# The sixteen experts' outputs in a fused vision/mixture kernel: one weighted running sum on VectorE instead of scaled copies on ScalarE and a tree of additions

## The reference

```python
logits = einsum('bsd,de->bse', x, gate_w) + gate_b
top_probs, top_idx = top_k(softmax(logits), 2)          # then divided by their sum
dispatch = sum(one_hot(top_idx, 16) * top_probs[..., None], axis=-2)   # 14 of 16 are zero
h1 = einsum('bsd,edh->bseh', x, w1)
h2 = einsum('bsd,edh->bseh', x, w2)
hidden = silu(h1) * h2                                  # 128 hidden units per expert
expert_out = einsum('bseh,eho->bseo', hidden, w3)
out = h + einsum('bseo,bse->bso', expert_out, dispatch) # x = layernorm(h)
```

## Time and profile before

| | us |
|---|---|
| median of 3 runs | 2467.79 (2460.09 to 2467.89) |
| the profiled execution, its own time | 2476.72 |
| its span, first to last instruction | 2474.9 |
| mean granted TensorE clock | 0.943 |

### The profile page before, as it was taken

One profiled execution on the slowest core, in us unless ns is written; L12 is line 12 of the kernel. 1 busy time (PEld: TensorE's weight loads), 2 busy tenths in 40 slices (PEclk: granted clock), 3 DMA queues, 4 the chain that ended last, 5 costly groups with the idle time before them and its releaser, 6 DMA issues.

```text
span 2474.9 us, 46859 instructions
## 1 busy us (share of the span) xinstructions
PE 2210.1 (89%) x15441; PEld 1979.4 (80%) x15441; DVE 1856.8 (75%) x4865; ACT 1399.1 (57%) x4344; POOL 1673.7 (68%) x2168
## 2 busy tenths in 40 slices
PE   2578989989999998999999899999999999989887
PEld 1566778888888888879889888888889888878776
DVE  1226888788788778888787878878787888887765
ACT  1124466566665656566565656656565666655555
POOL 0378887777686858868586877858686786867500
PEclk9967999999999999999899999989999999989989
DMA  9575636356472736538272745638173563712100
GB/s 221 148 207 154 182 104 186 113 164 173 110 217 66 213 97 177 167 106 222 77 212 85 198 138 152 186 95 225 52 221 108 166 175 109 201 52 68 49 3 6
DMA packets 362993, 346.85 MB, mean 140 GB/s; under 512 B 49152, under 2 KB 313472, under 8 KB 362624
## 3 DMA queue, kind: packets, MB, share of 16 engines
q1 hardware_dynamic: 313600, 209.57, 31.4%
q0 software_dynamic: 49152, 134.28, 18.6%
HBM read 205.87 MB, written 137.89 MB: 139 GB/s over the span
## 4 chain that ended last, share of the span: by engine, by line
PE 58%; issue 11%; DVE 11%; ACT 10%; POOL 8%; DMA 2%; ACTq 0%; DVEq 0%; another core or an unknown queue 0%; POOLq 0%
PE bank_o L634 16%; PE bank_h L624 8%; PE bank_d L700 7%; PE bank_h L625 7%; PE bank_d L690 7%; POOL gath L570 5%; ACT scaled L831 5%; PE bank_a L727 5%; PE bank_a L712 2%; POOL rest L577 2%; DMA gath<-table,idx 2%; DVE hid L967 2%; DVE wsam L1062 1%; PE bank_p L655 1%; PE bank_a L741 1%
## 5 line engine op out<-in xcount | busy, mean ns | idle before, releaser
L570 POOL DMA_INDIRECT gath<-table,idx x1024 | 1110.6, 1085 | 267.2 <-issue 238.5
L831 ACT ACTIVATE scaled<-bank_o,disp 128x64 f32<-128x64 f32 x2304 | 502.2, 330 | 370.8 <-PE bank_o L634 334.4
L624 PE MATMUL bank_h<-xsplit,w 128*128 128x384 f32 x1536 | 634.7, 413 | 83.3 <-ACT silu L780 52.9
L634 PEld LDWEIGHTS bank_o<-w_sb,hid 128*128 128x128 f32 x4608 | 567.9, 197 | 10.1 <-DVE hid L967 9.6
L634 PE MATMUL bank_o<-w_sb,hid 128*128 128x64 f32 x4608 | 563.8, 278 | 6.3 <-DVE hid L967 6.2
L625 PE MATMUL bank_h<-xsplit,w 128*128 128x384 f32 x1536 | 539.0, 351 | 0.0
L780 ACT ACTIVATE silu<-bank_h 128x384 f32<-128x384 f32 x768 | 393.8, 514 | 122.0 <-PE bank_h L625 104.2
L967 DVE TENSOR_TENSOR hid<-silu,bank_h 128x384 f32<-128x384 f32 x768 | 416.8, 548 | 53.4 <-ACT silu L780 38.5
L577 POOL MEMSET rest<- 1x400 f32 x1024 | 432.1, 422 | 29.6
L624 PEld LDWEIGHTS bank_h<-xsplit,w 128*128 128x128 f32 x1536 | 307.6, 200 | 139.5 <-ACT silu L780 68.0
L1062 DVE TENSOR_TENSOR wsam<-gath,cw 128x1024 f32<-128x1024 f32 x256 | 312.6, 1221 | 115.4 <-PE bank_d L690 54.7
(11 more groups left out here) (141 smaller groups left out, 2306.2 us busy)
## 6 DMA issues: line engine op xcount, KB each, us to landing
table<-pixmaj SPq DMA_DIRECT2D x80, 1024.0 KB
xin<-x_dram SPq DMA_DIRECT2D x256, 256.0 KB
table<-pixmaj SPq DMA_DIRECT2D x32, 960.0 KB
table<-pixmaj SPq DMA_DIRECT2D x16, 1088.0 KB
gath<-table,idx POOLq DMA_INDIRECT x1024
out_dram<-ob SPq DMA_DIRECT2D x48, 96.0 KB
gath<-w_dram SPq DMA_DIRECT2D x4, 512.0 KB, 8.8
interp_sb<-interp_dram SPq DMA_DIRECT2D x1, 1024.0 KB, 5.3
```

The costliest lines, as they stand in the source:

```text
L570: pool.indirect_dma_start(out=gath[buf][:, p, :, :].rearrange("p a c -> p (a c)"), out_offset=None, in_=table[par], in_offset=bass.Indirec ...
L624: mm(bank[:, 0:GC], w12[:, e, which, 0, :], xsplit[gp][:], start=True, stop=False)
L634: last = mm(bank_o[n % 2][:, C * i:C * (i + 1)], hid[:, e, 128 * k:128 * (k + 1)], w3_sb[:, e, :], start=True, stop=True)
L831: last = nc.scalar.activation(scaled[n % 2][:, i, :], bank_o[n % 2][:, C * i:C * (i + 1)], ACT.Identity, scale=disp[gpar(par, g)][:, k, e: ...
```

## The change

Each expert's output is handled by itself. As soon as its `hid` is there, PE makes the three tiles' outputs (three products of 64 columns) in one bank, and DVE runs three instructions of 64 columns, one per tile: output from PSUM times the dispatch weight (one number per token, read from `disp`) plus the running sum `ob`, written back to `ob`; for expert 0 the residual `h2` stands in place of the running sum. ACT has no part in it any more. `scaled`, `part`, M2 and their semaphores are gone; `hid` holds 4 experts' products instead of 16; `eo_added` counts the additions. The order strings of all five engines are new.

```diff
+HB = 4
-    ("W", "pe"): [(0, 0, 0), (0, 0, 1), (0, 0, 2), (0, 1, 0), (0, 1, 1), (0, 1, 2), (1, 0, 0), (1, 0, 1), (1, 0, 2), (1, 1, 0), (1, 1, 1), (1, 1, 2), (2, 0, 0), (2, 0, 1), (2, 0, 2), (2, 1, 0), (2, 1, 1), (2, 1, 2)],
+    ("W", "pe"): [(i, j) for i in range(3) for j in range(16)],
...
 ORDER = {
     "pe": (
...
-        "kFhlFlFEEFvEFaxFaaFaFFaaFEFEkFrEFkFslFtlFakFaFakFElFvlFEkFxEkFalFalFakFEFkaFlFErlFsaFEkaFtaFkblFblFE",
+        "FEtEaFbbkFElFElFbEbvFEbkFExFkbEbFlEbFlEcFEkFEdkFElFErlFsEFkEFEtkgFEhlFElFEaFEvFaEaFExEFaaFEaFaEaFEFE",
...
-        hid = sb("hid", [128, NE, GC])
-        scaled = [sb(f"scaled{i}", [128, 8, C]) for i in range(2)]
-        part = sb("part", [128, 2, GT, C])
+        hid = sb("hid", [128, HB, GC])
...
                     elif kind == "W":
-                        g, half, k = args
-                        n = 2 * GT * (NGRP * b + g) + GT * half + k
-                        pe.wait_ge(hid_done, SLOTS * b + NE * g + 8 * half + 8)
-                        wait(pe, eo_scaled, n - 1)
-                        for i in range(8):
-                            e = 8 * half + i
-                            last = mm(bank_o[n % 2][:, C * i:C * (i + 1)], hid[:, e, 128 * k:128 * (k + 1)],
+                        g, e = args
+                        n = SLOTS * b + NE * g + e
+                        pe.wait_ge(hid_done, n + 1)
+                        wait(pe, eo_added, GT * (n - 1))
+                        for k in range(GT):
+                            last = mm(bank_o[n % 2][:, C * k:C * (k + 1)], hid[:, n % HB, 128 * k:128 * (k + 1)],
                                       w3_sb[:, e, :], start=True, stop=True)
                         last.then_inc(eo_ready, 1)
...
-                    elif kind == "W":
-                        act.wait_ge(eo_ready, n + 1)
-                        act.wait_ge(disp_done, NGRP * b + g + 1)
-                        wait(act, pair_sum, n - 1)
-                        for i in range(8):
-                            e = 8 * half + i
-                            last = nc.scalar.activation(scaled[n % 2][:, i, :], bank_o[n % 2][:, C * i:C * (i + 1)],
-                                                        ACT.Identity, scale=disp[gpar(par, g)][:, k, e:e + 1])
-                        last.then_inc(eo_scaled, 1)
...
-                        if e % 8 == 0:
-                            wait(dve, eo_ready, 2 * GT * (NGRP * b + g - 1) + GT * (e // 8 + 1))
+                        wait(dve, eo_ready, n - HB + 1)
                         r = (2 * (NE * g + e) + 1) % 3
-                        tt(hid[:, e, :], silu[e % 2][:], bank_h[r][:, 0:GC], ALU.mult).then_inc(hid_done, 1)
+                        tt(hid[:, n % HB, :], silu[e % 2][:], bank_h[r][:, 0:GC], ALU.mult).then_inc(hid_done, 1)
                     elif kind == "Z":
-                        dve.wait_ge(eo_scaled, n + 1)
-                        eo = scaled[n % 2]
-                        for m in (4, 2):
-                            link(sums, tt(eo[:, 0:m, :], eo[:, 0:m, :], eo[:, m:2 * m, :], ALU.add))
-                        tt(part[:, half, k, :], eo[:, 0, :], eo[:, 1, :], ALU.add).then_inc(pair_sum, 1)
-                    elif kind == "M2":
-                        dve.wait_ge(pair_sum, 2 * GT * (NGRP * b + g + 1))
-                        wait(dve, out_done[gp], 8 * NGRP * b + 8 * (g - gp))
-                        link(mix, tt(ob[gp][:], part[:, 0, :, :], part[:, 1, :, :], ALU.add))
-                        tt(ob[gp][:], ob[gp][:], h2[g][:], ALU.add).then_inc(ob_done, 1)
+                        dve.wait_ge(eo_ready, n + 1)
+                        if e == 0:
+                            wait(dve, out_done[gp], 8 * NGRP * b + 8 * (g - gp))
+                        for k in range(GT):
+                            if e:
+                                dve.wait_ge(eo_added, GT * (n - 1) + k + 1)
+                            stt(ob[gp][:, k, :], bank_o[n % 2][:, C * k:C * (k + 1)], disp[gp][:, k, e:e + 1],
+                                (ob[gp] if e else h2[g])[:, k, :], ALU.mult, ALU.add).then_inc(eo_added, 1)
```

More of the change, by code:

```diff
@@ L119 @@
     ("L", "sp"): [(i,) for i in range(8)],
-    ("M2", "dve"): [(i,) for i in range(3)],
     ("M2", "sp"): [(i,) for i in range(3)],
@@ L152 @@
     ("X", "dve"): [(i, j) for i in range(3) for j in range(16)],
-    ("Z", "dve"): [(0, 0, 0), (0, 0, 1), (0, 0, 2), (0, 1, 0), (0, 1, 1), (0, 1, 2), (1, 0, 0), (1, 0, 1), (1, 0, 2), (1, 1, 0), (1, 1, 1), (1, 1, 2), (2, 0, 0), (2, 0, 1), (2, 0, 2), (2, 1, 0), (2, 1, 1), (2, 1, 2)],
+    ("Z", "dve"): [(i, j) for i in range(3) for j in range(16)],
 }
@@ new lines @@
+        "GxFCGyFGFqGjFGFGjrFsGFGjFGlFGlFmGtjuFGFGwFGjlFGlvmFjGFGxFGyFGljFqGlFmGFGjrFsGFGlFjlGmAFGBjFGtFuGFGCl",
+        "wlFmGjFGvFjGFGxFyGqFGljFrsGlmFGjFGdFGeFljGFlgmGFGjFGtuFGilFGwlFmGAFGvFGGBFxFCGyFGFqGjFGFGjrFsGFGjFGl",
+        "FGlmFGtjuFGFGwjFGlFGlvmFjGFGxFGyFGljFqGlFmGFGjrFsGFGFljlGmFAGFGtujFGBFlGCwlFmGjFGvFGjFGxFGyFGlFqjGlF",
+        "mGFGrFsGjFGFGFGlFjGltmuFGFGwFjGFGvFGFGlxlFmGAyFGBFCGqFGFGrFsGFGFGFGFGtuFGFGwFGFGvFGFGxFGyFGFqGFGFGrF",
+        "sGFGFGFGFGtuFGFGwFGFGvFGFGxFGyFGFGFGFGFGFGFGFGFGFGFGFGFGFGFGFGFGFGGG",
@@ L241 @@
-        "DppoozopozoozoozDppoozopozoozoozDppoozopozoozzDppppppppp",
+        "ooDDoozoozoozoozoozoozoozoozoooooozzzoozpDoooopzzpoozopDozpoozoozpoozpoozDpoozoozpoozpoozDpoozoozpoo",
+        "zpoozDpoozoozpoozpoozDpoozoozpoozpoozDpoozoozpoozpoozDpoozoozpoozpoozDpoozoozpoozpoozDpoozoozpoozpoo",
+        "zDpoozoozpoozpoozDpoozoozpoozpoozDpoozoozpoozpzDpppppppp",
     ),
@@ L475, in gpar @@
             return (NGRP * p + g) % 2
-        def n_odd(g, half, k):
-            return (2 * GT * g + GT * half + k) % 2
         @block.sync
@@ L506, in out_group @@
             def out_group(b, g, gp):
-                wait(sp, ob_done, NGRP * b + g + 1)
+                wait(sp, eo_added, GT * NE * (NGRP * b + g + 1))
                 dst = out[b]
@@ L910, in _ @@
             step(ts(c_st[:], c_st[:], col[:, 13:14], None, ALU.mult))
-            nc.vector.memset(part[:], 0.0).then_inc(setup_done, 1)
+            nc.vector.memset(hid[:, 0, 0:8], 0.0).then_inc(setup_done, 1)
             dve.wait_ge(setup_a, 6)
@@ L920, in _ @@
                                   Chain(top_s, NGRP * TOP_N))
[L922 removed]
+            skip = Chain(skip_v, NGRP * 2)
             def link(chain, ins):
@@ L1005, in run @@
                         dve.wait_ge(skip_v, 2 * NGRP * b + 2 * g + 2)
-                        wait(dve, ob_done, NGRP * (b - 1) + g + 1)
+                        wait(dve, eo_added, GT * (SLOTS * (b - 1) + NE * g + 1))
                         tt(h2[g][:], bank_p[:, 0:GT * C].rearrange("p (k c) -> p k c", k=GT),
@@ L1045, in run @@
                         link(top, ts(top_p[:, 3, :], top_p[:, 1, :], -0.5, 0.5, ALU.mult, ALU.add))
-                        wait(dve, eo_scaled, 2 * GT * (NGRP * b + g - 1))
+                        wait(dve, eo_added, GT * NE * (NGRP * b + g - 1))
                         top.inc(tt(disp[gp][:], spread(iota_e[:], 1, GT), spread(top_f[:, :, 0], 2, NE), ALU.is_equal))
```

167 lines of the change are left out of this document (78 added, 89 removed).

## The result

The changed kernel takes 2380.76 us (median of 4 runs, 2372.95 to 2384.32) against 2466.61 us of the kernel before (4 runs, 2460.09 to 2467.89): a ratio of 0.9653, 95% interval 0.9623 to 0.9682, or 86 us less. The forecast had the direction, but 31 us, and its range for the likeliest case (2405 to 2458) lies above the result; the wider range, 2380 to 2500, just holds it. The profiled execution took 2381.35 us and spans 2379.1, where the one before spans 2474.9.

The account below looks back on a forecast made before the run. PE was taken to bound the middle, and waits, not an engine, the tail. Middle -31 + 6 + 17 = -8 us and tail -23 gave -31 from the median 2467.8, so 2437 us; range 2380 to 2500.

Parts of the forecast that it names:

- The step that failed: Middle, PE: 79 more transitions from an output product to an expert step, 0.08 us each, +6 us.
- ACT's term: Middle: scaled copies gone, half of PE's waits for silu and the `v_sb` copy saved, -31 us (bounds 0 and 63).
- DVE's price: Weighted addition of 64 columns on DVE: lasts 0.284 us, 0.20 start to start (0.145 to 0.31); DVE busy about 2010.
- the wait for `eo_ready`: DVE before each set of additions, waiting for PE's products: little or none; above 7 us per image meant wrong.
- the second term that failed: Middle, DVE: +9.7 us work less 8.5 us waiting per image, +17 us at worst if all reached PE.
- The tail: After the last D3 product: 128.4 us shrinks to 105, -23 us (bounds -35 and 0).
- The clock term: End of the run: clock averaging 0.89 in the last 127 us adds 14 us to 84 us of work.
- ACT busy: Whole run, a sign to check: ACT busy about 900 us.
- Line 1142's successor: Middle, once-per-image line: expected every 141 to 142 us; under 139 meant the forecast was wrong.
- A: Whole kernel, the forecast itself: silu and evacuations prompt, DVE has room; 2405 to 2458 us, chance 0.46.
- D: Middle: PE's waits nearly vanish, an image takes 134 to 137 us; whole kernel 2335 to 2376 us, chance 0.14.
- C: Whole kernel: nothing moves, ACT's waits were hidden, DVE's longer list eats the end's gain; 2461 to 2475 us, chance 0.12.

Follow-up runs that it names:

- e2_act_copies: Changed kernel with ACT's three scaled copies per expert put back and one 192-column addition per expert on DVE: 2389.42 us, ratio 0.9677.
- e4b_act_filler_waits: Changed kernel plus three unused 64-column ACT instructions per expert, each set waiting for that expert's products on PE: 2445.07 us, ratio 0.9901.
- e4a_act_filler: Changed kernel plus three unused 64-column ACT instructions per expert, without a wait for PE's products: 2392.74 us, ratio 0.9693.
- b1_one_copy: Kernel before, old order, each round's eight scaled ACT copies replaced by one 512-column copy without dispatch weights: 2428.32 us, ratio 0.9836.
- c2_pairs: Changed kernel with two experts' outputs in a row on PE and their six additions in a row on DVE, eight `hid` buffers: 2430.74 us, ratio 0.9817.
- c4_fours: Changed kernel with four experts' outputs and their twelve additions in a row, 16 `hid` buffers, two experts per bank: 2554.77 us, ratio 1.0371.
- b2_no_act_copy: Kernel before, old order, no output copies on ACT; dispatch weights and half the outputs left out, DVE reads PSUM: 2441.14 us, ratio 0.9885.
- e5_dve_filler: Changed kernel plus one more weighted addition of 64 columns per expert on DVE, into a scratch tile: 2472.43 us, ratio 1.0035.
- h2_act_copies_later: e2_act_copies with each set of scaled copies 1.0 us later in ACT's string: 2434.42 us, ratio 0.9869 against the kernel before.

## Why the forecast was right and wrong, step by step

The chain before, e2_act_copies, e4b_act_filler_waits, changed takes the change apart: first the order and the size of the sets (ACT's copies stay; DVE's work becomes 53 us less); then the additions go to DVE (+211 us of DVE work, ACT about as loaded and still waiting for the products); then ACT's share goes away. Per image and for the tail, by the table:

| step | 13.8 images | of it with the clock (estimate) | tail | whole, by the ratios | forecast |
|---|---|---|---|---|---|
| order, small sets | -3.5 x 13.8 = -49 | +5 | -30 | -80 | +6 in the middle |
| additions on DVE | +3.7 x 13.8 = +51 | +20 | +2 | +55 | +17 in the middle |
| ACT free | -4.3 x 13.8 = -59 | -38 | -3 | -61 | -31 in the middle |
| sum | -57 | -13 | -32 | -86 | -8 and -23 |

The column on the clock comes from PE's time per image over the same eleven images, with the same products in each. The trace's clock record has two levels, full and half; half of PE's busy time at the half level is what that level costs at most. It is an estimate, and what sets the level isn't shown.

| us per image | PE idle | half of its busy time at the half level | the rest | image |
|---|---|---|---|---|
| before | 8.4 | 5.2 | 128.6 | 142.1 |
| e2_act_copies | 6.7 | 5.5 | 126.4 | 138.6 |
| e4b_act_filler_waits | 8.2 | 6.9 | 127.2 | 142.3 |
| e4a_act_filler | 6.8 | 4.8 | 127.3 | 138.9 |
| changed | 6.7 | 4.2 | 127.1 | 138.0 |
| b1_one_copy | 6.5 | 6.0 | 127.5 | 140.0 |
| c2_pairs | 7.5 | 4.3 | 128.5 | 140.3 |
| c4_fours | 11.5 | 5.6 | 129.7 | 146.9 |

**The step that failed** is that the new order was priced only by its 79 further transitions on PE ("79 x 0.08 = +6 us"). Taken by itself it is the largest term of the three, -80 us. It isn't the clock's doing, which is no higher in e2_act_copies (0.946) than before (0.949). Part of it is the 53 us by which DVE's own work fell; at the slopes measured for DVE (0.18 to 0.67) that is 10 to 36 us, which leaves 44 to 70 for the order. The runs bear on it from both sides: with ACT relieved but the rounds kept, the gain is 28 to 40 us (b2_no_act_copy, b1_one_copy); with ACT free and the sets doubled or quadrupled, 41 us and 177 us are lost (c2_pairs, c4_fours).

**ACT's term** (-31, half of its bound of 63) came out as -61 in this sequence, of which some 38 go with the clock (0.940 in e4b_act_filler_waits, 0.960 changed), and as -28 to -40 in the old order. Without the clock it is near its forecast. The rows that it was read from were right: PE's wait for silu fell from 37.3 to 0.8, below the 20 that I had named.

**DVE's price** was right to 4%: 0.193 us from start to start for a forecast 0.20, busy 2011.2 for 2010. The single instruction lasts 0.275 (0.284). That the wait for `eo_ready` would cost little was right (7.4 us in 1500). What the work costs was not, the second term that failed: +17 forecast, +55 measured in the chain, some 20 of it with the clock. The forecast offset DVE's busy time against the 89.7 us it had waited for the copies; but PE now waits for DVE in three places, `ob`, `hid` and `wsam`, 56.5 us together in 1500, where before it waited 6.2 for `hid` at a step and nothing for sums.

A model price for this instruction was weighed ahead of the result. The trace has 0.193 us; the estimate of 142 ns by the Trainium skill's "Vector Engine (DVE) Microarchitecture Reference", section 5.2, is 51 ns below it, and 2304 of them would be off by 118 us. The rule to minimize the number of operations, in the Trainium skill's "VectorE: DVE Perf Modes", "Rules for kernel authors", is borne out as a cost (960 instructions became 2304, +154 us on DVE, and e5_dve_filler shows what such microseconds are worth here), yet the count didn't decide: e2_act_copies has 768 additions on DVE and a ratio of 0.9677, the changed kernel 2304 and 0.9653.

**The tail** was nearly right in size, and partly by luck: 96.5 us for 105. Both engines have what was forecast, PE 83.5 of 95 us and DVE 81.5 for "some 83" each. But the forecast had put it down to DVE's wait for ACT's copies foremost, and taking the copies off ACT isn't what shortened it: of its 32 us 30 come with the order, as e2_act_copies has 98.4 with ACT loaded, and b2_no_act_copy 115.3 with ACT free. (The order strings hold 53 sets of outputs there, not 54; that is 0.6 us.) The clock term was smaller than taken: 0.92 mean in the last 95 us, where it was 0.89.

**The head** had no term. Its 8 us are not tested by a run of their own, and it varies between the kernels here from 490 to 523 us.

**ACT busy** is 940.7, not 900: the forecast subtracted the copies' 502 us, and the engine's busy time fell by 458. **Line 1142's successor** comes every 138.0 us, not 141 to 142, below the 139 that I had named as a sign of being wrong.

**The rivals.** None came as drawn. The result, 2380.8 us, lies between A's range (2405 to 2458) and D's (2335 to 2376), nearer to D, the large gain with a chance of 0.14; but in D an image takes 134 to 137 us and PE's waits nearly vanish, where an image takes 138.0 and PE's idle time fell from 8.4 to 6.7 us of it. C and D both took PE's busy time of the kernel before as what an image needs at least. It isn't. From the fourth image's table to the fifteenth's, before, e2_act_copies, e4b_act_filler_waits, changed, c4_fours:

```profile
499.40:2062.90 1563.50, 1471.07 (x10618) 1331.72 (x10616) 1265.79 (x3323) 957.33 (x2981) 1152.47 (x1485) 0.96 0.54 151
```

```profile
502.90:2027.60 1524.70, 1450.67 (x10621) 1345.29 (x10620) 1229.12 (x3192) 991.67 (x2982) 1149.50 (x1487) 0.96 0.56 155
```

```profile
511.20:2076.40 1565.20, 1475.37 (x10619) 1358.77 (x10620) 1376.49 (x4248) 1044.09 (x2983) 1158.34 (x1487) 0.95 0.54 151
```

```profile
491.60:2010.00 1518.40, 1444.43 (x10619) 1334.35 (x10620) 1372.51 (x4247) 641.84 (x1400) 1160.36 (x1487) 0.97 0.55 155
```

```profile
517.00:2132.30 1615.30, 1488.39 (x10615) 1332.09 (x10615) 1389.30 (x4247) 634.41 (x1399) 1170.67 (x1487) 0.96 0.52 146
```

For the same products PE is busy 133.7 us per image before (1471.07 / 11), 131.9 in e2_act_copies, 134.1 in e4b_act_filler_waits, 131.3 in the changed kernel and 135.3 in c4_fours. Of the 4.1 us that the change takes off an image, 2.4 lie inside what the trace calls busy and 1.7 are idle time. At most 0.9 of the 2.4 go with the clock, which is at its half level for 11.2 us of an image before and 8.7 now; 1.5 are left. Since the profile models the ends of matmuls, what these 1.5 are can't be read from it.

**The clock** had no term in the middle. Among the 42 executions of the kernel before, each compared with those beside it, a mean granted clock 0.01 higher goes with a time 10 us shorter; with 0.949 on the mean before and 0.960 in the changed kernel that is an estimate of 11 us out of the 86, close to the 13 of the table. Why the clock is higher isn't shown: it doesn't simply follow the stalls, since h2_act_copies_later has 0.963 and takes 2434 us, with more idle time of PE than the kernel before.

**What stays open.** The order and the size of the sets changed together in the kernel; c2_pairs and c4_fours move the size and, with it, the place of the first outputs by one to three steps. I tried no kernel with old places and small sets. In both the row of products on PE grows with the row of additions on DVE, so which of the two rows costs the time isn't shown either. And small sets by themselves don't make PE's busy time small: e4b_act_filler_waits has them and the largest busy time but one of these five.

## What to carry to other kernels

Before pricing the instructions that a change adds and removes, look at how long a row each engine runs for one purpose, against the period of the work that must pass between: rows of 2.6 us on VectorE, with as many products in a row on TensorE, against a step of 2.96 cost more than all that the freed ScalarE gave. A busy share of the bounding engine is no floor; compare its busy time for the same work between kernels first, and look at the granted clock of both. And price an engine's extra work by the slope at its present load: here 0.67 us per us upwards and 0.18 downwards.
